# A decoder block on one core: the first and last steps of each engine written out in orders of their own, and a new repeating order between them

## The reference, cut to what matters

```python
x = _layernorm(x + attn(x))            # 16 heads of 16; two gained layer norms feed q and kv; rotary scaled by |x|;
                                       # layer norm per head of q and k; causal softmax; output projection
x = _layernorm(x + xattn(x, ctx))      # each sequence as a 64 x 256 matrix, transposed: 8 heads of 8 over 256 positions,
                                       # band |i-j| <= 64, softmax; o = relu(out projection) * ctx; second projection
x = _layernorm(x + ffn(x))             # weights quantised to {-1,0,1} x scale by groups of 64;
                                       # h = silu(gate) * up (1024 wide); rms norm; projection back to 256
```

## Time and profile before

| | us |
|---|---|
| median of the three runs | 999.11 |
| the profiled execution | 996.99 |
| its span, first to last instruction | 995.1 |
| PE busy | 920.1 (92%) |
| DVE busy | 852.5 (86%) |
| ACT busy | 805.7 (81%) |
| POOL busy | 789.4 (79%) |

### The profile page before, as it was taken

One profiled execution on the slowest core, in us unless ns is written; L12 is line 12 of the kernel. 1 busy time (PEld: TensorE's weight loads), 2 busy tenths in 40 slices (PEclk: granted clock), 3 DMA queues, 4 the chain that ended last, 5 costly groups with the idle time before them and its releaser, 6 DMA issues.

```text
span 995.1 us, 26660 instructions
## 1 busy us (share of the span) xinstructions
PE 920.1 (92%) x10614; PEld 569.7 (57%) x10614; DVE 852.5 (86%) x1719; ACT 805.7 (81%) x1395; POOL 789.4 (79%) x1133
## 2 busy tenths in 40 slices
PE   5878898999999999999999999999999999998985
PEld 2344455556666666666666666666666665664553
DVE  4799888988999999999999999999998998877653
ACT  2554677788899888888898899888888988887865
POOL 2765798989988888888899888888888898745642
PEclk8989999999999999999999999999999999998998
DMA  7000000000000000000000000000000000000000
GB/s 246 7 12 16 19 18 18 18 18 18 8 18 19 23 24 14 22 24 23 24 24 24 13 23 24 23 24 13 23 24 23 23 19 18 18 13 13 28 12 22
DMA packets 24827, 24.75 MB, mean 25 GB/s; under 512 B 4992, under 2 KB 23680, under 8 KB 24704
## 3 DMA queue, kind: packets, MB, share of 16 engines
q1 hardware_dynamic: 24704, 23.05, 8.1%
HBM read 14.12 MB, written 4.19 MB: 18 GB/s over the span
## 4 chain that ended last, share of the span: by engine, by line
PE 57%; DVE 25%; POOL 7%; ACT 7%; issue 2%; SPq 1%; DMA 1%; POOLq 0%; DVEq 0%; ACTq 0%
DVE rowmax L1406 6%; PE ps L615 6%; PE ps L581 5%; PE ps L595 5%; DVE q_rows L1397 4%; ACT high L896 4%; PE ps L491 4%; PE ps L512 4%; DVE k_rows L1397 3%; PE ps L458 3%; PE ps L421 3%; PE ps L437 3%; PE ps L527 3%; POOL hsum L1129 3%; PE ps L605 3%; PE ps L394 2%
## 5 line engine op out<-in xcount | busy, mean ns | idle before, releaser
L1406 DVE TENSOR_REDUCE rowmax<-ps 128x4 f32<-128x768 f32 x256 | 243.2, 950 | 38.4 <-PE ps L491 37.2
L911 ACT ACTIVATE prob<-ps 128x768 f32<-128x768 f32 x256 | 207.9, 812 | 21.6 <-PE ps L512 21.2
L1129 POOL TENSOR_TENSOR hsum<-hsum,minus_half 128x32 f32<-128x32 f32 x32 | 174.5, 5455 | 30.3 <-DVE hsum L1349 30.3
L1152 POOL TENSOR_SCALAR_AFFINE_SELECT prob<-prob 128x256 f32<-128x256 f32 (+1 forms) x256 | 140.3, 548 | 28.3 <-ACT prob L911 28.3
L1154 POOL TENSOR_SCALAR_AFFINE_SELECT prob<-prob 128x512 f32<-128x512 f32 (+1 forms) x256 | 137.5, 537 | 0.0
L896 ACT ACTIVATE high<-ps,bx_col 128x512 f16<-128x512 f32 x128 | 89.2, 777 | 21.3 <-PE ps L458 21.3
L491 PE MATMUL ps<-k_rows,q_rows 24*128 24x192 f16 x1024 | 87.4, 249 | 18.6 <-DVE rowmax L1406 14.8
L527 PE MATMUL ps<-prob,v_pad 128*32 128x192 f32 x2048 | 103.8, 332 | 0.4 <-POOL prob L1154 0.3
L512 PE MATMUL ps<-q_rows,k_rows 25*128 25x192 f16 x1024 | 87.0, 248 | 2.8 <-ACT prob L911 1.7
L491 PEld LDWEIGHTS ps<-k_rows,q_rows 24*128 24x128 f16 x1024 | 30.7, 93 | 85.2 <-issue 32.9
L527 PEld LDWEIGHTS ps<-prob,v_pad 128*32 128x32 f32 x2048 | 57.0, 109 | 38.7 <-issue 26.6
(11 more groups left out here) (159 smaller groups left out, 2369.6 us busy)
## 6 DMA issues: line engine op xcount, KB each, us to landing
v_swap<-v_own SPq DMA_DIRECT2D x64, 68.0 KB, 2.3
xin<-in_x SPq DMA_DIRECT2D x32, 128.0 KB, 2.1
enc<-in_ctx SPq DMA_DIRECT2D x32, 128.0 KB, 2.2
out<-yout SPq DMA_DIRECT2D x32, 128.0 KB, 1.9
prob<-in_w_guT SPq DMA_DIRECT2D x4, 512.0 KB, 7.4
prob<-in_w_projT SPq DMA_DIRECT2D x2, 512.0 KB, 9.9
q_rows<-in_Wkv SPq DMA_DIRECT2D x1, 512.0 KB, 5.2
wx_qk<-in_wx_qk SPq DMA_DIRECT2D x1, 512.0 KB, 4.6
```

Of the source, the lines that this page charges most:

```text
L911: copy(prob[:, 2 * c:2 * c + 2, :, :].rearrange("p u a b -> p u (a b)"), ps[:, STB:STB + 2, 0:2 * QW], ACT.Exp, scale=float(XD) ** -0.5).t ...
L1129: g.tensor_tensor(hsum[:, 1, :], hsum[:, 0, :], minus_half[:, :], ALU.pow).then_inc(S["head_pow3"], 1)
L1152: g.affine_select(out=lead, in_=lead, compare_op=ALU.is_ge, fill=0.0, base=BAND - 64 * kb, pattern=[[0, 4], [1, cut]], channel_multiplier=-1)
L1406: v.tensor_reduce(of_head[:, hq:hq + 2, 2 * ng:2 * ng + 2], ps[:, MXB:MXB + 2, 0:2 * QW].rearrange("p j (a b) -> p j a b", a=2), AX, ALU.m ...
```

## The change

Every operation is split into `do_` (the work) and `put_` (its waits, then `do_`). `steps` now covers numbers 10 to 39 only. What the engines do before step 10 and after step 39 is written out operation by operation with its own waits, in an order that is not that of the step; many waits that another wait implies are left out. POOL is different: its lags are counted from 10 on, so nearly all of its start runs in the repeating order, and only its end is written out.

```diff
-LAST_LAG = 17
+FIRST_STEP, LAST_STEP = 10, 40
...
-    for number in range(TILES + LAST_LAG):
+    for number in range(FIRST_STEP, LAST_STEP):
         step(Step(number))
```

The banks of several stages change (PE; the readers follow):

```diff
-                    last = tr(ps[:, MXB + 1, 128 * i:128 * i + 128], xn[:, 128 * i:128 * i + 128], ident[:, :])
+                    last = tr(ps[:, G7, 128 * i:128 * i + 128], xn[:, 128 * i:128 * i + 128], ident[:, :])
...
-                    last = mm(ps[:, MXB + 1, 0:DIM], xnT[:, i, :], wqkv[:, i, 512:768], start=i == 0, stop=i == 1)
+                    last = mm(ps[:, G6, 0:DIM], xnT[:, i, :], wqkv[:, i, 512:768], start=i == 0, stop=i == 1)
...
-                    last = tr(ps[:, G5, 128 * i:128 * i + 128], qkn[:, 128 * i:128 * i + 128], ident[:, :])
+                    last = tr(ps[:, G7, 128 * i:128 * i + 128], qkn[:, 128 * i:128 * i + 128], ident[:, :])
...
-                    last = mm(ps[:, (MXB, G6)[c], :], xsplitT[:, i, :], wgu[:, i % 2, 512 * c:512 * c + 512], start=i == 0, stop=i == 3)
+                    last = mm(ps[:, G6, :], xsplitT[:, i, :], wgu[:, i % 2, 512 * c:512 * c + 512], start=i == 0, stop=i == 3)
...
-                    last = mm(ps[:, MXB + 1, 0:256], hT[:, i // 8, i % 8, :], wproj[:, i % 8, :], start=i == 0, stop=i == 15)
+                    last = mm(ps[:, G7, 0:256], hT[:, i // 8, i % 8, :], wproj[:, i % 8, :], start=i == 0, stop=i == 15)
```

The start on PE begins so:

```diff
+            pe.wait_ge(S["xn"], tile[0].at(1, 1))
+            do_xnT_ps(tile[0])
+            sum_gains()
+            pe.wait_ge(S["xnT"], tile[0].at(1, 1))
+            do_qk_ps(tile[0])
+            turn_bias()
+            sum_weights(0)
+            do_v_ps(tile[0])
+            pe.wait_ge(S["xn"], tile[1].at(1, 1))
+            do_xnT_ps(tile[1])
...
+            do_qkT_ps(tile[0])
+            carry_bias()
+            sum_weights(2)
+            keep_warm(3)
```

and on DVE so, with the 24 parts of the quantising spread over the whole start (the last one stands between tile 5's `attn` and tile 3's `max` 3):

```diff
+            do_x_stats(tile[0])
+            dve.wait_ge(S["x_pow"], tile[0].at(1, 1))
+            do_xn_nb(tile[0])
+            spread_gains()
+            scale_weights()
+            fold_bias()
+            dve.wait_ge(S["qk_ps"], tile[0].at(1, 1))
+            do_qk(tile[0])
+            scale_gains()
...
+            do_x_stats(tile[1])
+            hold_bias()
+            dve.wait_ge(S["rotated"], tile[0].at(1, 1))
+            do_centred(tile[0])
...
+            quantise(0, 1)
+            dve.wait_ge(S["squared"], tile[0].at(1, 1))
+            do_variance(tile[0])
+            quantise(0, 2)
```

The written-out start holds 66 `keep_warm` matmuls. The end on PE is short:

```diff
+            pe.wait_ge(S["y3"], tile[29].at(1, 1))
+            do_up_ps(tile[31], 0)
+            do_gate_ps(tile[31], 1)
+            pe.wait_ge(S["h_lo1"], tile[30].at(1, 1))
+            do_hT_ps(tile[30], 1)
+            pe.wait_ge(S["hid0"], tile[31].at(1, 1))
+            do_up_ps(tile[31], 1)
+            pe.wait_ge(S["hid1"], tile[31].at(1, 1))
+            pe.wait_ge(S["hT1"], tile[30].at(1, 1))
+            do_down_ps(tile[30])
...
+            do_hT_ps(tile[31], 0)
...
+            do_down_ps(tile[31])
```

More of the change, by code:

```diff
@@ L214, in build @@
         names = """aT aT_ps attn centred ct_ps down_ps enc exp gate_ps0 gate_ps1 gated hT0 hT1 hT_ps0 hT_ps1 h_hi h_lo1 head_pow3
[L215 to L220, removed]
+                   heads0 heads1 hf hf_ps hid0 hid1 hid_pow high0 high1 high2 high3 max maxT_ps max_hi maxrow mx o_ps ot0 ot1 out
+                   proj_ps2 proj_ps3 pt0 pt1 pt_ps0 pt_ps1 qk qkT qkT_ps qk_ps qkn rotated rows0 rows1 rows2 rows3 s_exp s_max
+                   s_ps s_sub sel silu1 sqsum squared st tanh0 tanh1 tr_ps0 tr_ps1 up_ps0 up_ps1 v v_ps val variance vpad
+                   vproj_ps vswap wo_ps x1 x1_nb x2 x2_hi x2_lo x2_nb xT xT_ps x_pow x_stats xbo xload xn xnT xnT_ps xn_nb y1
+                   y1_pow y1_stats y2 y2_pow y2_stats y3 y3_pow y3_stats yout yout_nb z_ps zr attn_c centred_c heads_c variance_c
+                   x_stats_c y1_stats_c y2_stats_c y3_stats_c rotated_c eps0 eps1 eps2 eps3 eps_hid"""
         S = {n: sem("c_" + n) for n in names.split()}
@@ new lines, in _ @@
+            do_s_ps(tile[2])
+            pe.wait_ge(S["xnT"], tile[4].at(1, 1))
+            do_qk_ps(tile[4])
+            keep_warm(3)
+            pe.wait_ge(S["s_sub"], tile[2].at(1, 1))
+            do_proj_ps(tile[0], 1)
+            pe.wait_ge(S["rows0"], tile[0].at(1, 1))
+            do_mx(tile[0], 0)
+            do_proj_ps(tile[0], 3)
+            keep_warm(3)
+            pe.wait_ge(S["max"], tile[0].at(8, 1))
+            do_mx(tile[0], 1)
+            keep_warm(2)
+            pe.wait_ge(S["qkn"], tile[3].at(1, 1))
@@ new lines, in _ @@
+            keep_warm(1)
+            pe.wait_ge(S["sel"], tile[0].at(4, 1))
+            do_val(tile[0], 0)
+            pe.wait_ge(S["qkT"], tile[4].at(1, 1))
+            do_vproj_ps(tile[1])
+            pe.wait_ge(S["attn"], tile[3].at(1, 1))
+            do_aT_ps(tile[3])
+            pe.wait_ge(S["exp"], tile[0].at(8, 4))
+            do_st(tile[0], 4)
+            pe.wait_ge(S["max"], tile[1].at(8, 5))
+            do_mx(tile[1], 5)
+            pe.wait_ge(S["vpad"], tile[1].at(1, 1))
+            do_xnT_ps(tile[6])
@@ L1105, in _, with do_x_pow @@
             pool.wait_ge(s_pads, 7)
[L1106 to L1109 removed]
+            def do_x_pow(t):
                 g.tensor_scalar(base[:, 0, :], mv[:, 0, 1:2], EPS, None, ALU.add).then_inc(S["eps0"], 1)
```

2764 lines of the change are left out of this document (2044 added, 720 removed).

## The result

The changed kernel takes 966.92 us (median of 4 executions, 965.52 to 972.07), the kernel before on the same chip 998.32 (4 executions). The ratio is 0.969, with a 95% interval of 0.966 to 0.973: faster by 31 us, where 20 were forecast.

A forecast was written before the change was run, and what follows sets the result against it. The prediction took PE to bound the step, with DVE half a microsecond behind. Gains of 9 (start), 8.4 (repeating part) and 3 (end) took 996.99 to 976.6, plus 2.1 for the median: 979 us, range 962 to 1003.

The forecast's parts named there:

- all three gains: Start, repeating part and end gain 9, 8.4 and 3 us in about this size; 968 to 989 us, chance 0.50.
- DVE's amount of work after 21 us: Start: DVE's 194.8 us busy falls to 191.8, as about 3 us move ahead of 21 us; gain 9.
- my density of 0.905: Start: assumed DVE busy share, between today's 0.881 and the repeating part's 0.922, giving 212 us.
- That lead of 12 to 14 us: Start: the first power begins near 23 us instead of 36.79; a lead forecast as not all kept.
- Fillers at nothing: Start: 56 fewer `keep_warm` matmuls, 15 us on PE, costed at nothing because DVE's pace hides them.
- rival C: Clock: fewer fillers lower the start's granted clock, and half-speed stretches may enter the repeating part; 991 us, chance 0.08.
- The pairs of `st` and `mx`: Repeating part, PE: seven pairs side by side instead of six, 0.43 us against 0.27 each alone; -0.1 per step.
- my walk: Repeating part: one step followed wait by wait; PE work 26.45 plus waits 0.4 gives 26.85, taken as 26.8 us.
- A: Repeating part: the step stays at 27.2 us; 987 us, chance 0.18.
- B: POOL between `zr` and next `gated`: slack of 1.1 us turns negative and the step lengthens; 1013 us, chance 0.14.
- the longer case: Repeating part: ten uses of bank G7 bring a half-speed stretch in every third step, 10 us more.
- D: Start: its lead is given back because DVE is as loose as before; 987 us, 995 with a loss, chance 0.10.

The follow-up runs named there:

- e3: Changed kernel, but DVE quantises the first weights before it takes tile 0's `qk`, as the kernel before did; 978.3 us, ratio 0.977 to 0.985.
- e11: Changed kernel without the third part of each weight quantising, 8.3 us less DVE work in the start; 964.9 us, ratio 0.963 to 0.970.
- e4: Kernel before, with tile 0's layer norm, `xnT`, `qk`, rotation, centring and variance ahead of the first weights' quantising; 995.2 us.
- e2: Changed kernel with its first steps run from the loop in the new steady order, and 32 instead of 66 filling matmuls; 999.6 us.
- e5: Same as e2, but with the 122 filling matmuls of the kernel before; 999.3 us, ratio 0.999 to 1.004.
- e10: Changed kernel with 132 filling matmuls in place of 66, each call doubled; 967.6 us, ratio 0.965 to 0.972.
- e6: Changed kernel without any filling matmul (66 fewer); 976.8 us, ratio 0.974 to 0.980.
- e7: Changed kernel with DVE's `h_lo1` behind maximum 3 instead of ahead of it; 970.2 us, ratio 0.968 to 0.973.
- e9: e7 plus maximum 4 ahead of the centring on DVE, and ACT's squares behind the `v_pad` copy and the tanh of half 1; 963.1 us.
- e12: e9 plus DVE's `heads` 1 ahead of the `y3` statistics and ACT's squares behind the copies of `hT` 1 and `hf`; 962.6 us.
- e1: Changed kernel with every engine's last steps run from the loop instead of written out; 971.3 us, ratio 0.970 to 0.977.

## Why the prediction was right, and where its terms were off

The time lies in the range (962 to 1003) and in the likeliest case, all three gains. Summed like the forecast, 996.99 - 21.9 - 7.5 - 0.8 = 966.8, and the profiled execution took 966.67; the forecast's 976.6 is 10 off: the start brought 13 more, the end 2 less and the steps 1 less.

**The start: direction right, size off by 13.** The step that failed is DVE's amount of work after 21 us, "about 3 us of that [...] move ahead of 21 us, leaving 191.8". It measured 183.0. The new order reaches tile 10's `xnT` with less of DVE's work done, 183.0 + 9.8 up to there against 194.8 + 6.2 before, and does it later: the repeating part and the end have 539.9 + 134.5 busy where the earlier trace rows has 528.2 + 123.2. By count, 12 of DVE's instructions have changed from the start to the end, seven row maxima and four row copies among them, 10 us in sum. In the repeating part the count is the same, 1092, and of its 11.7 us more the longer `h_lo1` makes 16.9, less 5.2 of others. At my density of 0.905 these 8.8 us are 9.7 of the 12.8 that were missing; the other 3.1 are density, which came out at 183.0/199.2 = 0.919. The model itself was weak too. "That lead of 12 to 14 us is not all kept, since DVE has a fixed amount to do" is contradicted by e3, where 9.9 of 10.2 us are kept, and by e11, where 8.3 us less work give 4.1. The start is rather a chain of tiles; e4 shows that a lead of tile 0 alone is mostly lost, and the change gives one to tile 1 too. How the remaining 12.2 us (229.9 in e3 against 242.1) divide between hand-written order and new steady order, e2 and e5 leave open.

**Fillers at nothing.** "DVE's pace hides them" holds from 66 upwards (e10, 0.6 us). The margin was smaller than the step made it sound: e6 lost 9.9 us without the rest. This is rival C's mechanism, a start with less clock; the change itself kept 0.94 where the earlier trace rows has 0.95.

**The step: 26.92 for 26.8, by two errors that cancel.** Of the 7.5 us of this stretch 5.3 are the step's 0.25 (26.92 for 27.17); the kernel before also lost 1.5 to its half-speed stretch there, and its first step (27.67) and two others (27.37, 27.27) were longer. I had PE's work 0.05 us shorter and its waits 0.3 shorter. In ten whole steps PE is busy 262.8 of 269.2 us, against 266.4 of 271.7 before: work is 0.36 shorter and idle time 0.1 longer. Each step after lacks the records of two matmuls of `gate` and `up`, and PE's idle time inside these two groups, 0.10 us, is new; it is the record's. So the waits are as long as before (0.54 against 0.53) and the work is 0.26 shorter.

The pairs of `st` and `mx` are part of that, but not as forecast. In the kernel before six pairs are neighbours and five run together, two of them at once, in 0.35 us where one alone takes 0.34, and three 0.12 to 0.18 us apart, in 0.46 to 0.50. "An `st` and an `mx` side by side take 0.43 us" (up to what follows) was read from one of these three. After, six run together, five of them at once, and the seventh stands one behind the other. Up to the start of what follows, all `st` and `mx` take 0.59 us less of a step, the split `proj` groups 0.20 more, and the rest is spread over other neighbours. At once in the kernel before, then at once and one behind the other after:

```profile
529.11 0.26 PE L491 MATMUL ps<-k_rows,q_rows 24*128 24x192 f16 x2
529.12 0.26 PE L512 MATMUL ps<-q_rows,k_rows 25*128 25x192 f16 x2
```

```profile
449.10 0.26 PE L570 MATMUL ps<-k_rows,q_rows 24*128 24x192 f16 x2
449.11 0.26 PE L601 MATMUL ps<-q_rows,k_rows 25*128 25x192 f16 x2
...
451.22 0.34 PE L570 MATMUL ps<-k_rows,q_rows 24*128 24x192 f16 x4
451.56 0.34 PE L601 MATMUL ps<-q_rows,k_rows 25*128 25x192 f16 x4
```

What my walk missed is the wait of `hT` 1 for maximum 4, 0.62 us; it took the place of the waits that `mx` lost. It was missed because I took DVE's work from the order before ("the same operations"), and `h_lo1` beside POOL's addition is not the same duration: 0.8 us more ahead of maximum 4. e7 shows that this alone decides nothing, e9 and e12 that the wait was to be had.

**Rivals.** A, no gain in the step, is out: 26.92 to 26.95 in every run that keeps the order. B, POOL's ring: its wait at `gated` is 1.01 us where I had 1.1, POOL is busy 94% of a step (531.9 of 565.3), and the ring does not close; even in e12, with 0.40 left there, it doesn't. C: the granted clock of the repeating part is 1.00 with ten uses of G7 per step, so the longer case did not come. The rule of the Trainium skill, "TensorE: Matmul & The Clock Gate", section "A second HAM failure mode: psum-queue depth-cycling", would have had the clock swing there, as the prediction applied it; the trace does not agree. D is refuted by the start's own 21.9 and by e3.

**The end: -0.8 for -3.** The waits that the forecast named are gone, the 1.15 us of `tr` 1 for `hid` and the 0.17 of `z`; tile 31's `ct` waits 1.37 for `gated` instead. The written-out order took no wait away (e1). Two things hide in the number. The cut at tile 31's `xnT` hides some: from tile 10's `xnT` to tile 0's `down` it is 9.5 us after and 6.1 before, so the end now holds 3.4 us more of a tile's way. Counted like that the end gained 4, and the start 3.4 less. But the clock explains that much by itself: it was granted 0.98 where the earlier trace rows has 0.94, about 6 us at half speed against 20, and at the price of the earlier trace rows these 14 us are some 6 us of time (an estimate, if nothing hides them). The prediction had no term for the clock in the end. e4, with the old steps, has 0.92 there, and the runs with the new steps 0.97 to 0.99; which part of the change does this, no run tells.

## What to carry to other kernels

When a hand-made order starts a pipeline, look at when the second item enters, not only the first; a lead of one item alone is lost in the next one's place in line. When an order is changed, re-read the durations of what has become neighbours on engines that share a way to memory, and after every exchange ask which instruction, unrelated to the wait, stands behind the one that waits. Before a few microseconds between two traces are given to an order, compare their waits one by one and their granted clock. Fillers that look free under another engine's pace have a lower bound that is worth measuring before they are thinned out.

## What the hardware showed that was not expected

- DVE's `scalar_tensor_tensor` over 128x1024 with two SBUF inputs takes 1.28 us, and 2.07 when it starts 1 us ahead of the end of a POOL `tensor_tensor`; a POOL `tensor_scalar` of one element behind it takes 1.19 instead of 0.22. POOL's power of 128x32 does not do that: one-column instructions of DVE with two SBUF inputs took 0.15 and 0.22 during its 5.47 us.
- 66 filling matmuls of 0.38 us each are worth 10 us of 967, 7.3 of it by tile 7's `xnT` at 145 us, and 66 more are worth nothing.
- An `mx` group (24 rows) and an `st` group (25 rows) that start together take 0.35 us, one alone 0.34; started 0.12 to 0.18 us apart they take 0.46 to 0.50.
